# Gate stage with its routing folded in, last expert stage per tile with the norm inside, branch sums on VectorE

## What is computed

```python
stats = concatenate([_stats(t) for t in (local_short, local_long, delta_out, v_direct)], -1)  # mean, var, mean |.|, l2 of 32
gin = concatenate([hs_exp, stats], -1)                       # 128 + 16 per token and head, 4 heads
logits = gelu(gin @ gW1 + gb1) @ gW2 + gb2
probs = softmax(logits / exp(log_temp), -1)
probs = probs * (1.0 - sum(floor, -1)) + floor
o = probs[0]*local_short + probs[1]*local_long + probs[2]*delta_out + probs[3]*v_direct
o = o + sigmoid(conv_res_logit) * local_short + alpha_id * (hs @ Wid)
o = o * rsqrt(mean(o * o, -1) + 1e-05) * o_norm_w
x = layernorm(x + o @ Wo)
# (d): the one chosen expert of each token
logits = x @ gate_w + gate_b;  pb = softmax(logits);  e = argmax(pb)
out = layernorm(x + pb[e] * (gelu(x @ w1[e] + b1[e]) @ w2[e] + b2[e]))
```

## Time and profile before

| | us |
|---|---|
| median of 3 runs (1529.28 to 1536.52) | 1529.68 |
| the profiled execution | 1537.19 |
| its span | 1535.0 |
| engine busy: PE, DVE, ACT, POOL | 1000.4, 841.9, 588.0, 336.7 |
| TensorE clock granted, mean | 0.742 |

### The profile page before, as it was taken

One profiled execution on the slowest core, in us unless ns is written; L12 is line 12 of the kernel. 1 busy time (PEld: TensorE's weight loads), 2 busy tenths in 40 slices (PEclk: granted clock), 3 DMA queues, 4 the chain that ended last, 5 costly groups with the idle time before them and its releaser, 6 DMA issues. The chain is left out here.

```text
span 1535.0 us, 34540 instructions
## 1 busy us (share of the span) xinstructions
PE 1000.4 (65%) x13068; PEld 766.8 (50%) x13069; DVE 841.9 (55%) x2298; ACT 588.0 (38%) x1111; POOL 336.7 (22%) x351
## 2 busy tenths in 40 slices
PE   6776787767719999245563948855777664505950
PEld 2454555545619999123232747753456433505950
DVE  3655667756435555178775851115767774212436
ACT  1444444444405555265664221103344433103530
POOL 0111321333324444345331011000000000061025
PEclk9888888878559999577676967655665576557985
DMA  3202222122412221222322141130121110711213
GB/s 93 48 16 53 67 53 59 40 62 64 149 45 62 60 60 51 81 76 71 74 56 45 42 63 18 19 80 20 42 76 41 48 42 14 254 40 52 68 48 96
DMA packets 182433, 93.86 MB, mean 61 GB/s; under 512 B 63534, under 2 KB 173969, under 8 KB 182176
## 3 DMA queue, kind: packets, MB, share of 16 engines
q1 hardware_dynamic: 175904, 79.37, 20.5%
q0 software_dynamic: 6400, 12.67, 2.6%
HBM read 56.72 MB, written 35.79 MB: 60 GB/s over the span
## 5 line engine op out<-in xcount | busy, mean ns | idle before, releaser
L1515 ACT ACTIVATE bx_h<-bx_up,bx_cur 128x128 f32<-128x128 f32 x288 | 82.1, 368 | 101.2 <-PE bx_up L1494 101.2
L617 ACT ACTIVATE a_at<-a_scores 128x1024 f32<-128x1024 f32 x64 | 65.3, 1021 | 113.1 <-PE a_scores L468 113.1
L463 PE MATMUL a_scores<-a_rk,a_kx 32*128 32x128 f32 (+3 forms) x1024 | 64.3, 329 | 59.2 <-DVE a_at L809 56.4
L538 POOL TENSOR_TENSOR a_vx<-a_vx,a_con 128x2048 f32<-128x2048 f32 x8 | 36.2, 4522 | 286.5 <-DMA a_vx<-lion_values 286.5
L1456 POOL DMA_INDIRECT chosen_b<-bx_ys,bx_to x72 | 74.2, 1031 | 97.5 <-DVE bx_ys L1544 95.7
L463 PEld LDWEIGHTS a_scores<-a_rk,a_kx 32*128 32x128 f32 x1024 | 48.3, 222 | 85.4 <-DVE a_at L809 70.1
L1494 PE MATMUL bx_up<-bx_xT,bx_cur 128*128 128x128 f32 x576 | 81.8, 286 | 2.5 <-DVE bx_cur L1529 2.5
L1476 PE MATMUL bx_down<-bk_w,bx_h 128*128 x576 | 81.9, 286 | 0.4 <-ACT bx_h L1515 0.4
L1494 PEld LDWEIGHTS bx_up<-bx_xT,bx_cur 128*128 128x128 f32 x576 | 70.9, 194 | 9.2 <-DVE bx_cur L1529 4.2
L530 POOL DMA_INDIRECT regions_b<-a_xo,a_seat x64 | 63.6, 994 | 49.3 <-DVE a_seat L781 28.1
L1476 PEld LDWEIGHTS bx_down<-bk_w,bx_h 128*128 128x128 f32 x576 | 69.7, 191 | 2.9 <-issue 0.8
(11 more groups left out here) (397 smaller groups left out, 2650.2 us busy)
## 6 DMA issues: line engine op xcount, KB each, us to landing
a_vx<-lion_values SPq DMA_DIRECT2D x32, 256.0 KB, 5.1
bx_xs<-regions_b SPq DMA_DIRECT2D x72, 65.0 KB, 1.8
bk_w<-in_b_w SPq DMA_DIRECT2D x16, 256.0 KB, 5.8
...
```

The source lines that it names most:

```text
L463: mm(S4[:, g, o:o + P - 32 * q], kx[rows, 0, 4 * t + q].rearrange("p h j -> p (h j)"), rk[b][rows, 0, t * P + 32 * q:(t + 1) * P], start=T ...
L617: op(at[m % 2][:], S4[:, :, 0:320].rearrange("p g (q k) -> p g q k", q=2)[:, :, :, 0:P], ACT.Copy).then_inc(s_ata, 1)
L1515: i = op(h[u % 2][:, f, :], BU[u % 2][:, f * P:(f + 1) * P], act_fn, bias=cur[u % 2][:, FC * P + f:FC * P + f + 1])
```

## The change

It replaces the end of the program from `gate_stage` on.

1. `delta_project` no longer writes the normed rows for the gate stage; it writes them already turned (`xT_rows`, 128 x 4096), which the gate stage loads as it is. The residual is no longer turned on PE.
2. `gate_stage`, still a step per group, is written anew. DVE takes the branch statistics without centering (three passes of 2048: sum L2248, sum of ACT's squares L2252, sum of magnitudes L2253), multiplies by the probabilities in one instruction of 2048 (L2333), and sums the branches in two halving additions (1024 and 512 wide, L2336 and L2337) on DVE. Logits: 4 matmuls with the second gate matrix as weights and 512 columns moving (L2003), a scaling copy on ACT (L2161), 4 matmuls of 16 columns (L2007). Reciprocal roots are powers on POOL (L2067, L2073): of 64 values for the norms, 16 for the root mean square, 4 for the layer norm. The layer norm's output is written by ACT (L2173).
3. Layer (d)'s gate product is 8 more columns of the output projection (L2044, L2047); for group n-1, each step picks the expert (L2275 to L2291), counts (PE L2014, L2016), finds the seats (L2297 to L2304), and POOL scatters the rows of group n-2 (L2108, 4 indirect writes). The tile table and the pad rows follow at the end of the stage, as in `lion_stage` (now the function `tile_table`, L127). The expert weights of (d) are loaded during the first steps.
4. `moe_stage` is gone. `expert_stage` "d" runs 40 tiles; with `norm` set, ACT does `fetch` (L1053), DVE adds result and residual and takes their moments (L1092 to L1103), POOL computes the reciprocal deviation (L988, L990) and writes the normed rows to the output with an indirect write per tile (L994). There is no combine.

Core of the diff (the DVE and ACT lists of a step, and the expert stage):

```diff
+            def deviation(j, u):
+                pool.wait_ge(s_z, j + 1)
+                nc.gpsimd.tensor_scalar(vr[:, u:u + 1], mv[:, u, 1:2], LN_EPS, None, ALU.add).then_inc(s_vr, 1)
+                pool.wait_ge(s_vr, j + 1)
+                nc.gpsimd.tensor_tensor(rsv[:, u:u + 1], vr[:, u:u + 1], power[:], ALU.pow).then_inc(s_rs, 1)
...
+            def fetch(j, u):
+
+                e = act.value_load(expert[0:1, bass.ds(j, 1)], min_val=0, max_val=NE - 1)
+                op(cur[u % 2][:], w1[:, bass.ds(e, 1), :].rearrange("p e c -> p (e c)"), ACT.Copy).then_inc(s_cur, 1)
...
+                if norm:
+                    dve.wait_ge(s_b, j + 1)
+                    v.scalar_tensor_tensor(z[u][:], yb[u % 2][:], xs[u][:, P + 1:P + 2], xs[u][:, 0:P], ALU.mult, ALU.add
+                                           ).then_inc(s_res, 1)
+                    dve.wait_ge(s_res, j + 1)
+                    v.bn_stats(bst[:, u, :], z[u][:]).then_inc(s_bn, 1)
+                    dve.wait_ge(s_bn, j + 1)
+                    after(dve, s_st[u], g * 16)
+                    v.tensor_copy(to[u][:], xs[u][:, P:P + 1])
+                    v.bn_aggr(mv[:, u, :], bst[:, u, :]).then_inc(s_z, 1)
+                    return
                 after(dve, s_st[u], g * 16)
...
+            def normed(j, u):
+                dve.wait_ge(s_rs, j + 1)
+                v.tensor_scalar(ys[u][:], z[u][:], mv[:, u, 0:1], rsv[:, u:u + 1], ALU.subtract, ALU.mult).then_inc(s_y, 1)
...
+            def logits(m):
                 for h in range(NH):
+                    pe.wait_ge(s_hid, 4 * m + h + 1)
+                    i = mm(S[32 * h:32 * h + 32, :], gw2[:], hid[:, h, :], start=True, stop=True, skip_group_check=True)
+                i.then_inc(s_lt, 1)
+                pe.wait_ge(s_lgT, m + 1)
+                for t in range(GT):
+                    i = mm(S[:, t * NH * NA:(t + 1) * NH * NA], lgT[:, tiles[t]], C["sel16"], start=True, stop=True)
+                i.then_inc(s_lp, 1)
...
+            def norms(m):
+                pool.wait_ge(s_ssq, m + 1)
+                if m:
+                    pool.wait_ge(s_stp, m)
+                op.tensor_tensor(st4[:, :, :, 3], ssq[:], powers[:, 0:1].unsqueeze(1).broadcast_to([P, NA, TH]), ALU.pow
+                                 ).then_inc(s_l2, 1)
...
+            def mixed_deviation(n):
+                pool.wait_ge(s_ms, n + 1)
+                then(op.tensor_scalar(msp[:], ms[:], 32.0 * LN_EPS, None, ALU.add))
+                power(rms[:], msp[:], 1, TH).then_inc(s_rms, 1)
...
+                v.tensor_reduce(st4[:, :, :, 0], X[b][:], AX_X, ALU.add).then_inc(s_s0, 1)
+                dve.wait_ge(s_sq, m + 1)
+                if m:
+                    dve.wait_ge(s_l2, m)
+                v.tensor_reduce(ssq[:], xc[:], AX_X, ALU.add).then_inc(s_ssq, 1)
+                v.tensor_reduce(st4[:, :, :, 2], X[b][:], AX_X, ALU.add, apply_absolute_value=True)
+                dve.wait_ge(s_s0, m + 1)
+                v.scalar_tensor_tensor(msq[:], st4[:, :, :, 0], 1.0 / 32, st4[:, :, :, 0], ALU.mult, ALU.mult).then_inc(s_msq, 1)
+                dve.wait_ge(s_msq, m + 1)
+                v.tensor_tensor(st4[:, :, :, 1], ssq[:], msq[:], ALU.subtract).then_inc(s_st, 1)
...
-                for a in range(NA):
-                    i = own.mark(v.tensor_tensor(mix[:, a], X[b][:, a], wide(pr[:, :, a], 32), ALU.mult))
-                dve.wait_ge(s_dve, i)
-                then(v.tensor_reduce(o[:], mix[:].rearrange("p a j c -> p j c a"), AX_X, ALU.add))
+                v.tensor_tensor(mix[:], X[n % 2][:], pr[:].rearrange("p j a -> p a j").unsqueeze(3).broadcast_to([P, NA, TH, 32]),
+                                ALU.mult).then_inc(s_mix, 1)
+                dve.wait_ge(s_mix, n + 1)
+                then(v.tensor_tensor(half[:], mix[:, 0:2], mix[:, 2:4], ALU.add))
+                then(v.tensor_tensor(osum[:], half[:, 0], half[:, 1], ALU.add))
                 dve.wait_ge(s_id, n + 1)
-                v.tensor_tensor(o[:], o[:], B[2].rearrange("p (j c) -> p j c", c=32), ALU.add).then_inc(s_o, 1)
-                if not last:
-                    variances(n + 1)
+                if n:
+                    dve.wait_ge(s_on, n)
...
-    stage(delta_stage, [x1, chosen[0:TOK], chosen[TOK:]], x2, x3, v_rows, s_rows, pick("c"), ins["consts"])
-    stage(moe_stage, "d", x3, out, d_sorted, d_results, pick("d"), ins["consts"], 1, ACT.Gelu, True)
+        stage(expert_stage, "b", regions, chosen, route, keep, NT_TOP2, ACT.Relu, ins["consts"], False)
+    stage(delta_stage, [x1, chosen[0:TOK], chosen[TOK:]], xT_rows, d_rows, l_rows, v_rows, s_rows, pick("c"), ins["consts"])
+    with ExitStack() as ctx:
+        keep, route = expert_tables(nc, ctx, "d", pick("d"), regions_d, NT_TOP1)
+        stage(gate_stage, d_rows, l_rows, v_rows, s_rows, xT_rows, pick("c"), ins["consts"], route)
```

More of the change, by code:

```diff
@@ L1511, in body @@
                     j = g * U + u
+                    if norm and (u < U - 1 or not last):
+                        after(act, s_h, j)
+                        fetch(j + 1, (u + 1) % U)
                     act.wait_ge(s_up, j + 1)
@@ L2344, in _ @@
[L2344 to L2354 removed]
+            load_branches(1)
+            load_x(1)
+            load_x(2)
+            sp.wait_ge(s_padr, 1)
@@ L2483, in _ @@
-            square(0)
-            norms(0)
-            statistics(0)
-            steps(act, step)
-            sum_deviation(NG - 1)
+                if n:
+                    act.wait_ge(s_pj, n)
+                op(oc[:], I, ACT.Copy).then_inc(s_oc, 1)
+            top_exps(NG - 2)
+            norm(NG - 1)
+            top_exps(NG - 1)
         @block.vector
```

1111 lines of the change are left out of this document (438 added, 673 removed).

## The result

The changed kernel takes **1458.0 us** (median of 4 runs, 1457.0 to 1461.0); the kernel before, run beside it, 1529.5. The ratio is 0.953 (95% interval 0.950 to 0.956). The change is faster, by 71 us and not by the 138 of the forecast, and 1458 lies above the range of 1362 to 1434. The profiled execution took 1461.0 with a span of 1459.0, to be set beside the 1537.2 and 1535.0 of the kernel before.

What follows compares the result with a forecast made beforehand. The prediction took a loop of hand-overs between engines, not one full engine, to bound the gate step. Gate stage and routing 111 us less plus experts and combine 28 less, 139, scaled by 0.995, gave 1391 us; range 1362 to 1434.

Steps and rivals of the forecast that it cites:

- No row has a power: Gate step, POOL's round trip for the mean square: an addition and a power of 16 values put at 0.75 us.
- at most 3 a step if it takes 8: Gate step, POOL's power of 64 values for the norms: costed at nothing, at most 3 us a step.
- the lead: Gate stage from its first transfer to the first logits: 36 us.
- the steps: Gate stage's seven periods: a first of 20 us, then six of 24.5, together 167.
- the end: Gate stage's last step and routing, up to the next stage's first transfer: 55 us.
- the experts: Expert stage: 40 tiles of 2.45 us set by ACT, with start and end 111 us.
- The rival at 0.3 us per value: Gate stage: POOL computes powers value by value, about 20 us more every period, 139 in seven, say 1550; chance 0.01.
- 3 + 2 us of cover: Gate step: 3 us between square sums and statistics' end, 2 more behind PE's hidden layer, hiding the 64-value power.
- The high end: Top of the range: slow PE 22 us, slow expert tile 18 and POOL's powers 3 added to 1391, giving 1434.
- PE stays slow: Gate stage: column groups do not overlap or PE's clock stays low; step 27.7, 22 us more, 1413; chance 0.18.
- The loop closes sooner: Gate stage and experts: high clock, step 22.7, expert tile 2.3, 18 us less, 1373; chance 0.06.
- POOL and DVE block each other: Gate stage: POOL's moments operations fall behind DVE's multiplication of 2.3, 16 us more over seven steps, 1407; chance 0.06.

Runs made afterwards that it cites:

- all_products: Against the changed kernel, all powers of the gate stage on POOL (64, 16, 4 and 4 values) replaced by products; ratio 0.886 to the kernel before.
- norms_product: Against the changed kernel, only POOL's power of 64 values for the norms replaced by a product; ratio 0.911 to the kernel before.
- square_first: Against the changed kernel, ACT's square of the mixed rows moved ahead of the next group's gelus, same work; ratio 0.944 to the kernel before.
- norms_on_act: Against the changed kernel, the norms' 64 roots moved from POOL to ACT as a square root; ratio 0.922 to the kernel before.
- both_on_act: Norms' roots on ACT, PE counts and ACT's register read earlier, plus the 16-value root on ACT with an early one-value root and DVE reciprocal; ratio 0.904.
- gelu_ahead: Against both_on_act, ACT's gelus of the next group put ahead of its norm rows of the group before; ratio 0.886 to the kernel before.
- no_early_load: Against both_on_act, the one-value square root meant to load ACT's table early left out; ratio 0.897 to the kernel before.

## Why the prediction was wrong

**The step that failed is one term:** "No row has a power. The nearest is POOL's 782 ns at best for 128 columns", from which two operations were put at 0.75, and the 64 values were "costed at nothing, at most 3 a step if it takes 8". They measure 3.2 and 10.6. From all_products (another chip), the powers cost 43.5 - 33.2 = 10.3 in the lead, 219.1 - 152.0 = 67.1 in the steps and 56.7 - 50.9 = 5.8 at the end: 83 us, PE's slower clock beside them included. The rest of the sum was too long by 23 (2.8 in the lead, 15 in the steps, 5 at the end). Net 60 in the gate stage, and with 1.9 of a later start and 1 in the experts that is the whole difference between 139 and the 76 by which the span fell.

**The bound was taken from the wrong row.** A width says nothing of an operation whose cost per value is another. The rival at 0.3 us per value named the right mechanism and gave it 0.01, on the argument that POOL's row had 6 ns per value; that row is a subtraction and a multiplication. The measured price is 0.16, between the two, nearer to the rival; the 0.3 itself stands in no row. The rival's 1550 was too high because its price was twice the measured one, and because the step to which it was added was 2.4 too long.

**The cover fits, the way does not.** By the prediction's own rule, 3 + 2 us of cover, a power of 10.6 adds 5.6 a step; norms_product gave back 5.0 (31.3 to 26.3, with POOL's held pair against it), all powers together 9.6. So "at most 3 a step" failed by the 8 us that it assumed for the power. But the way by which the first power reached DVE is not in the prediction: its list for ACT had the square nowhere. The square stands behind the gelus, and there the power met a DVE that had its own group's output ready (4.36 us; square_first shows it with no work changed, 1.5 a step). With the square first, the wait is for PE's counts behind the logits, which is the way that the prediction did describe.

**The high end was added up wrong.** It takes 3 us for POOL's powers, where "at most 3 a step" is 21 over seven steps. With 21 the range would have ended at 1452, still under the 1458 measured.

**What held:** the branch sums (1.22 and 0.69 against 1.23 and 0.69); the experts, 2.40 a tile in the rows shown against 2.45, set by ACT with the register read of 0.73 bare; the table load at 1.28 with the gelu 0.01 behind it. For the load the trace was followed against the page "ScalarE: Activation LUTs", "What ACT_TABLE_LOAD costs", of the Trainium skill, rightly: no run here shows its drain of 1.38 between a load and the activation behind it. The third load of norms_on_act decides nothing on this, as it ran in a wait.

**What came out right by luck:** the end, 55.6 against 55. The powers cost 5.8 there and the rest was 5 too long.

**The rivals.** "PE stays slow": the four column-group matmuls end 2.0 behind the last gelu (1219.7 to 1221.7), near the 1.7 taken, at a mean clock of 0.66 over the seven periods; it did not decide. "The loop closes sooner": 21.7 in the kernel without powers, with the clock at 0.77. "POOL and DVE block each other": right, but not in the changed kernel. There the pair comes behind the long power, after DVE's multiplication, and its median is 0.21 and 0.24; only in the last step, which has no long power, is it held (1.88 and 1.20, from 1298.03). Once the long power is gone it is held in most steps, 2.6 us each, and stands on the chain by ACT's order. Taking it off gave 16 us over seven steps between both_on_act and gelu_ahead (167.9 to 151.5), or 14.7 on one chip (no_early_load's 166.2). That this is the rival's 16 is chance: the edit does not end the hold, it takes 4.84 us of wait and 1.50 of norm rows out of the gelus' way. The rule of the Trainium skill that stands with the rival, "SBUF — State Buffer", "SBUF: two separate sides", is borne out by the rows of the pair, which end with the DVE operations beside them, and not by those of the powers: by it DVE's multiplication, begun at 1206.43 inside the power of 1201.34 to 1211.96, would wait for the power's end, and it took its 2.29. There the measurement decides.
